# Attention contexts of a two-layer Flamingo block computed turned, four heads on column blocks of 32

## The reference

```python
x = x + tanh(g_xattn[0]) * L0_xattn(ctx, ctx, mask, layernorm(x), qc_score, ...)   # attention probabilities, 256 wide
x = x + tanh(g_ffn[0])   * L0_ffn(layernorm(x))      # shared expert + 8 experts, each run for all tokens, top 2 kept
x = x + tanh(g_xattn[1]) * L1_xattn(layernorm(x), ctx)
x = x + tanh(g_ffn[1])   * L1_ffn(layernorm(x))      # 8 experts, top 2 of 8
```

```python
scores  = einsum('bshr,bhlr->bhsl', q_r, k_r)          # queries and keys from folded weights
attn    = softmax(scores)                              # over the 256 latent rows l
ctx_c   = einsum('bhsl,bld->bhsd', attn, kv_rope)      # 64 values a head
ctx_lat = einsum('bhsd,hkd->bshk', ctx_c, w_kc_kv)
out     = ctx_lat.reshape(b, s, 16*128) @ Wo.T
```

## Time and profile before

| | |
|---|---|
| time, median of 3 runs | 470.16 us (469.36 to 470.41) |
| the profiled execution | 468.57 us, of which the span of the trace is 466.7 us |
| PE busy | 395.1 us, 85% of the span |
| PE's weight loads busy | 328.2 us, 70% |
| DVE busy | 261.4 us, 56% |
| ACT busy | 248.2 us, 53% |
| POOL busy | 135.8 us, 29% |
| mean granted TensorE clock | 0.955 of full speed |

### The profile page before, as it was taken

How to read it: one execution, slowest core, us unless ns; L and a number is a source line. 1 busy time by engine, 2 the same in 40 slices (tenths; PEclk the granted TensorE clock), 3 DMA queues, 4 the chain that set the end, 5 groups by cost and what they waited for, 6 DMA issues and landing times. The chain is left out here.

```text
span 466.7 us, 7900 instructions
## 1 busy us (share of the span) xinstructions
PE 395.1 (85%) x2691; PEld 328.2 (70%) x2691; DVE 261.4 (56%) x732; ACT 248.2 (53%) x507; POOL 135.8 (29%) x140
## 2 busy tenths in 40 slices
PE   1669994867988998898988898778998799999996
PEld 0335682456688777897778887678997677778885
DVE  0889434437623549624649433759762456555885
ACT  1013786437289466598484897543464354444331
POOL 4815100017001047011254011335178900001630
PEclk9999996958599999999999999999999899999999
DMA  5995700381001001020010100031264422211320
GB/s 156 303 328 186 103 2 0 117 266 44 2 23 25 2 22 25 2 47 1 1 46 3 24 23 2 1 97 47 63 204 145 146 89 73 90 46 58 103 91 23
DMA packets 30744, 35.37 MB, mean 76 GB/s; under 512 B 5713, under 2 KB 25793, under 8 KB 30449
## 3 DMA queue, kind: packets, MB, share of 16 engines
q1 hardware_dynamic: 26304, 28.11, 20.0%
q0 software_dynamic: 4400, 6.75, 6.4%
HBM read 25.61 MB, written 7.60 MB: 71 GB/s over the span
## 5 line engine op out<-in xcount | busy, mean ns | idle before, releaser
L1412 PE MATMUL bank<-kv,probs 128*128 128x128 f32 x512 | 67.6, 275 | 5.3 <-ACT negmT L1005 4.9
L1412 PEld LDWEIGHTS bank<-kv,probs 128*128 128x128 f32 x512 | 62.5, 192 | 6.2 <-issue 6.2
L1032 ACT ACTIVATE probs<-bank 128x512 f32<-128x512 f32 x64 | 37.5, 592 | 17.2 <-PE bank L1392 17.2
L1864 DVE TENSOR_REDUCE negm<-bank 128x2 f32<-128x512 f32 x64 | 41.4, 688 | 5.1 <-PE bank L1371 4.8
L1391 PE MATMUL bank<-Qs,Kh 128*128 128x256 f32 x128 | 39.0, 326 | 0.0
L1371 PE MATMUL bank<-Kh,Qs 128*128 128x256 f32 x128 | 32.3, 347 | 7.6 <-ACT fold_d L1015 3.0
L1574 PEld LDWEIGHTS bank<-W,hTs 128*128 128x128 f32 x210 | 28.1, 189 | 13.4 <-DVE hTs L2018 7.8
L936 ACT ACTIVATE gu_all<-bank 128x512 bf16<-128x512 f32 x44 | 25.9, 594 | 19.6 <-PE bank L1195 19.5
L1574 PE MATMUL bank<-W,hTs 128*128 128x256 f32 (+1 forms) x210 | 32.9, 293 | 3.8 <-DVE hTs L2018 2.6
L747 POOL TENSOR_TENSOR W<-w_in,W 128x512 fp32r<-128x512 f32 x24 | 30.0, 1279 | 21.2 <-issue 21.2
L736 POOL TENSOR_SCALAR veps<-mv 128x2 f32<-128x2 f32 x12 | 2.7, 225 | 111.2 <-DVE mv L1608 111.2
(11 more groups left out here) (209 smaller groups left out, 896.4 us busy)
## 6 DMA issues: line engine op xcount, KB each, us to landing
Qm<-Qs SPq DMA_DIRECT2D x32, 128.0 KB
xs<-f3A SPq DMA_DIRECT2D x1, 2432.0 KB, 10.2
Qm<-xs SPq DMA_DIRECT2D x19, 128.0 KB, 2.0
ys<-y SPq DMA_DIRECT2D x19, 128.0 KB, 2.0
w_q<-in_wq SPq DMA_DIRECT2D x2, 1024.0 KB, 17.8
w_o<-in_woT SPq DMA_DIRECT2D x1, 2048.0 KB, 11.2
w_in<-in_L_ffn_Wg SPq DMA_DIRECT2D x8, 256.0 KB, 4.6
w_in<-in_L_ffn_Wu SPq DMA_DIRECT2D x8, 256.0 KB, 3.1
```

The costliest lines, as they stand in the source:

```text
L1032: done(act.activation(flat(pT[:, n % 3]), bank1(b, FILL_ST + h)[:], ACT.Exp), "p_ready")
L1412: ins = pe.matmul(bank_v(b, h // 2)[:, at:at + P], pT[:, n % 3, lt, t * P:(t + 1) * P], kv_all[:, frm:frm + P], start=(lt == 0), stop=(lt ...
L1864: done(dve.tensor_reduce(negm[:, :, max_at(h)], rows(bank1(b, FILL_S + h)), AX.X, ALU.max, negate=True), "m_ready")
```

## The change

Contexts are computed turned. Exponentials now move, and the latent is stationary: for a quad of four heads, matmuls with 32 stationary columns go to output partitions 32k to 32k+31, one head k to each block. One round of them with a 128x32 block of ones gives each head's denominator, repeated on 32 partitions (`denominators(q)`); two rounds with the two halves of 32 of the latent's columns give the values (`values(q)`). A quad is 24 matmuls with 256 moving columns each. No transposes follow: DVE takes the reciprocal of 128x256 denominators into `rec`, multiplies 128x512 values with it and writes `full` in SBUF; ACT copies that once, into the high part. The second copy on ACT is gone; POOL (batch 3: DVE) makes the low part from `full`.

The quads stand at h5, h9, h13 and h17 on PE behind `scores_T` (the last denominators at h18 for batches 0 to 2), the reciprocal and the multiply at h6, h10, h14 and h18 on DVE, the high copy still at h7, h11, h15 and h19 on ACT. There are 6 buffers of exponentials in place of 3. Go, the folded output weights, is laid out by the same blocks: L1320 becomes 8 matmuls on blocks of 32 columns. In L1264 and L1265 the two heads of a pair now follow each other by operand (both first parts, then both second parts).

```diff
@@ PE: the fold
-                    for h in range(4 * q, 4 * q + 4):
-                        o = bank[4][half(h), h // 2 % 4 * KD:(h // 2 % 4 + 1) * KD]
-                        pe.matmul(o, w_qra[:, h], w_kqa[:, h], start=True, stop=False)
-                        ins = pe.matmul(o, w_qrb[half(h), h // 2], w_kqb[half(h), h // 2], start=False, stop=True)
+                    def o(h):
+                        return bank[4][half(h), h // 2 % 4 * KD:(h // 2 % 4 + 1) * KD]
+
+                    for pr in range(2 * q, 2 * q + 2):
+                        for h in (2 * pr, 2 * pr + 1):
+                            pe.matmul(o(h), w_qra[:, h], w_kqa[:, h], start=True, stop=False)
+                        for h in (2 * pr, 2 * pr + 1):
+                            ins = pe.matmul(o(h), w_qrb[half(h), pr], w_kqb[half(h), pr], start=False, stop=True)
...
-                    for j in range(2):
-                        for par in range(2):
-                            h = 2 * (2 * n + j) + par
-                            ins = pe.matmul(bank_go(n)[par * DC:(par + 1) * DC, j * H:(j + 1) * H], w_kv[:, h], w_o[:, h],
-                                            start=True, stop=True)
+                    for part in range(2):
+                        for k in range(4):
+                            ins = pe.matmul(bank_go(n)[QD * k:QD * k + QD, part * H:(part + 1) * H],
+                                            w_kv[:, 4 * n + k, part * QD:(part + 1) * QD], w_o[:, 4 * n + k], start=True, stop=True)
@@ PE: attn1
+                def in_quad(q, o, weights, sig):
+
+                    for lt in range(T):
+                        for k in range(4):
+                            ins = pe.matmul(o[QD * k:QD * k + QD], weights(lt), pT[(NH * b + 4 * q + k) % 6][:, lt],
                                             start=(lt == 0), stop=(lt == 1))
...
+                def denominators(q):
+
+                    pe.wait_ge(S_["p_ready"], NH * b + 4 * q + 4)
+                    if q:
+                        pe.wait_ge(S_["rec_ready"], NQ * b + q)
...
+                    in_quad(q, bank_den(b)[:, 0:S], lambda lt: ones[:], "den_ready")
+
+                def values(q):
+
+                    pe.wait_ge(S_["p_ready"], NH * b + 4 * q + 4)
...
+                    for part in range(2):
+                        in_quad(q, bank_v(b, q)[:, part * S:(part + 1) * S],
+                                lambda lt: kv[:, b * T + lt, part * QD:(part + 1) * QD], "pv_ready" if part else None)
...
-                    if 2 <= h <= NH + 1:
-                        values(h - 2)
-                    if h >= 7 and (h - 7) % 4 == 0:
-                        turn_ctx((h - 7) // 4)
+                    if h >= 5 and (h - 5) % 4 == 0:
+                        q = (h - 5) // 4
+                        if q < NQ - 1 or b == B - 1:
+                            denominators(q)
+                        values(q)
+                    if h == NH + 2 and b < B - 1:
+                        denominators(NQ - 1)
@@ ACT: attn1
-                        if n >= 3:
-                            act.wait_ge(S_["pv_ready"], n - 2)
+                        if n >= 6:
+                            act.wait_ge(S_["den_ready"], (n - 6) // 4 + 1)
+                            act.wait_ge(S_["pv_ready"], (n - 6) // 4 + 1)
...
-                        done(act.activation(flat(pT[:, n % 3]), bank1(b, FILL_ST + h)[:], ACT.Exp), "p_ready")
+                        done(act.activation(flat(pT[n % 6]), bank1(b, FILL_ST + h)[:], ACT.Exp), "p_ready")
...
-                        done(act.activation(flat(ctxs[:, 0, 2 * k:2 * k + 2]), bank_c(b)[:], ACT.Copy), "cT_hi")
-                        if b < B - 1:
-                            done(act.activation(wait_full(act, b, 4 + k), bank_c(b)[:], ACT.Copy), "cT_full")
+                        done(act.activation(flat(ctxs[:, 0, 2 * k:2 * k + 2]), full[k % 2], ACT.Copy), "cT_hi")
@@ DVE: attn1
-                    if h >= 3 and h % 2 and h <= NH + 1:
-                        pr = (h - 3) // 2
...
-                        done(dve.reciprocal(rden[:, m % 2], o[:, :, :, DC]), "pv_step")
-                        own(dve, "pv_step")
-                        done(dve.tensor_tensor(ctxn[:, :, 2 * pr:2 * pr + 2].rearrange("p t a d -> p a t d"), o[:, :, :, 0:DC],
-                                               rden[:, m % 2, :, :, None].to_broadcast([P, 2, T, DC]), ALU.mult), "ctx_ready")
+                    if h >= 6 and (h - 6) % 4 == 0:
+                        q = (h - 6) // 4
+                        m = NQ * b + q
+                        dve.wait_ge(S_["den_ready"], m + 1)
...
+                        done(dve.reciprocal(rec[:, m % 2], bank_den(b)[:, 0:S]), "rec_ready")
+                        dve.wait_ge(S_["pv_ready"], m + 1)
+                        own(dve, "rec_ready")
+                        done(dve.tensor_tensor(wait_full(dve, b, 4 + q).rearrange("p (a s) -> p a s", a=2),
+                                               bank_v(b, q)[:].rearrange("p (a s) -> p a s", a=2),
+                                               rec[:, m % 2, None, :].to_broadcast([P, 2, S]), ALU.mult), "ctx_ready")
```

More of the change, by code:

```diff
@@ L29 @@
 NP = NH // 2
+NQ = NH // 4
+QD = 32
 KD, CQ, R = 128, 192, 64
@@ L301, in passing @@
             return layer1.enter_context(nc.sbuf_tensor(name, shape, dt))
-        ctxn = passing("ctxn", [P, T, NH, DC])
+        probs_b = passing("probs_b", [P, 3 * T * S])
+        rec = passing("rec", [P, 2, S])
+        pT = [w[:, n * T * S:(n + 1) * T * S].rearrange("p (t s) -> p t s", t=T) for w in (probs, probs_b) for n in range(3)]
         ctxs = passing("ctxs", [P, 2, NP, S], F32R)
@@ L482, in wait_full, with bank_v, bank_den @@
                 pb, k = divmod(n, SPLITS)
-                if k < 4:
+                if k < 4 and pb < B - 1:
                     eng.wait_ge(S_["q_split"], 8 * pb + 2 * (k + 1))
+                elif k < 4:
+                    eng.wait_ge(S_["cT_lo"], NQ * pb)
                 else:
-                    eng.wait_ge(S_["cT_lo"], 4 * pb + k - 3)
+                    eng.wait_ge(S_["cT_lo"], NQ * pb + k - 3)
             return full[(SPLITS * b + i) % 2]
[L489 to L495, removed]
+        def bank_v(b, q):
+            return bank[(7, 4 if b < B - 1 else 3)[q % 2]]
+        def bank_den(b):
+            return bank[0 if b < B - 1 else 4]
         def qm_at(h):
@@ L789, in rotate @@
                 cv, rv, kvv = (w.rearrange("p (b t) c -> p b t c", b=B) for w in (cx, rot, kv))
-                done(pool.memset(kv[:, :, DC:DC + 1], 1.0), "rope_step")
-                done(pool.memset(kv_all[:, B * T * (DC + 1):], 0.0), "rope_step")
+                done(pool.memset(ones[:], 1.0), "rope_step")
                 done(pool.tensor_tensor(rv[:, :, :, 0:h2], cv[:, :, :, h2:DC], tab(sin, 0, h2), ALU.mult), "rope_step")
@@ L1393, in scores_T @@
                     done(ins, "sT_ready")
[L1395 to L1408, removed]
-                        for lt in range(T):
-                            at, frm = (h % 2 * T + t) * P, (b * T + lt) * (DC + 1)
-                            ins = pe.matmul(bank_v(b, h // 2)[:, at:at + P], pT[:, n % 3, lt, t * P:(t + 1) * P], kv_all[:, frm:frm + P],
-                                            start=(lt == 0), stop=(lt == 1))
-                    done(ins, "pv_ready")
-                def turn_ctx(k):
-                    pe.wait_ge(S_["ctx_ready"], NP * b + 2 * k + 2)
-                    if k:
-                        ctx_left(pe, 4 * b + k)
-                        if k == 3 and b < B - 2:
+                def in_quad(q, o, weights, sig):
+                    for lt in range(T):
+                        for k in range(4):
+                            ins = pe.matmul(o[QD * k:QD * k + QD], weights(lt), pT[(NH * b + 4 * q + k) % 6][:, lt],
+                                            start=(lt == 0), stop=(lt == 1))
+                    if sig:
+                        done(ins, sig)
+                def denominators(q):
+                    pe.wait_ge(S_["p_ready"], NH * b + 4 * q + 4)
+                    if q:
+                        pe.wait_ge(S_["rec_ready"], NQ * b + q)
+                        if q == NQ - 1 and b < B - 2:
                             pe.wait_ge(S_["fT0_sb"], b + 3)
@@ L1426, in turn_ctx @@
                         pe.wait_ge(S_["hsT_sb"], 2 * (b + 2))
-                    for j in range(2):
-                        for t in range(T):
-                            pr = 2 * k + j
-                            ins = pe.transpose(bank_c(b)[:, j * S + t * P:j * S + (t + 1) * P],
-                                               flat(ctxn[:, t, 2 * pr:2 * pr + 2]), ident[:])
-                    done(ins, "cT_ready")
+                    in_quad(q, bank_den(b)[:, 0:S], lambda lt: ones[:], "den_ready")
+                def values(q):
+                    pe.wait_ge(S_["p_ready"], NH * b + 4 * q + 4)
+                    if q == 0:
```

(11 more changed lines are left out.)

45 lines of the change are left out of this document (19 added, 26 removed).

## The result

The changed kernel takes 513.95 us (median of 4 runs, 512.5 to 514.76), the kernel before 469.76 us beside it: a ratio of 1.0963, 95% interval 1.0881 to 1.1044. The forecast was 489 us, with 507 as the upper end. The sign was right; the loss is 44 us in place of 19.

What follows compares the result with a forecast made beforehand. It took PE feeding ACT just in time to bound the loop, PE the down stage, a DVE chain the boundary. Terms of 15.85 us, 19.1 with the clock, took the profiled 468.57 to 487.7, median 489 us; range 463 to 507.

Steps and rivals of the forecast that it cites:

- Clock: PE's idle time before the down stage and fT0 widens; two half-speed stretches in all, 3.3 us (0 to 10).
- loop: Head loop, batches 0 to 2: ACT starves behind the quads at h5 and h9, +1.4 us a batch (-1.5 to +2.5).
- down stage and `y_sum`: Quad 2 falls in the PE-bound down stage, +1.05 us; its reciprocal and multiply on DVE delay `y_sum`, +2.2 us.
- boundary: Between batches: PE's values of quad 3 stand between fT0 and fT2 in place of later transposes, +0.1 us.
- high copy, queries, rows: Boundary: the last reciprocal and multiply follow `f2_lo` on DVE; ACT's high copy and query copies wait, +1.5 us.
- PE, a quad: PE's matmuls for one quad, four blocks abreast: 2.85 us, 1.1 us less than before.
- DVE, a quad: DVE's reciprocal of 128x256 for one quad: 2.0 us (0.42 to 1.95 from the rows), plus a 0.69 us multiply.
- Batch 3: +0.4: Last batch: PE's saving is hidden ahead of the scatter's landing; larger DVE pairs push the scatter 0.4 us (0 to 1.5).
- The fold: -1.7: Query fold L1264/L1265: paired halves save PE some 6 us, of which 1.7 us shows (0 to -2.3).
- PE sets the pace: Rival, 0.16: ACT stays fed through the quads and the reciprocal is near 0.42 us, so PE's saving counts: 455 us.
- blocks ran four abreast: Rival, 0.07, claimed they don't: a quad takes 5.4 us, 31 us more in 12 quads, some 520 us.
- reciprocal was not cheap: Rival, 0.20, claimed a cheap one: `y_sum` loses only 0.65 us, the queries nothing; 478 us, up to 480.

Runs made afterwards that it cites:

- a_filled: Changed kernel plus spare matmuls in PE's waits ahead of h3, h4, h5, h8, the down stage, fT0 and three row scores: 499.87 us.
- a_filled_b3: Changed kernel with spare matmuls in PE's waits, also in the last batch (ahead of its queries, h2 to h5 and the output): 494.42 us.
- a_oldfold: Changed kernel with the query fold L1264/L1265 back in its former head-by-head order: 514.84 us.
- a_spread_cheap: Changed kernel with each quad's rounds on three heads (last quad of a batch whole) and a copy for the reciprocal: 481.95 us.
- b_filled2: Kernel before plus spare matmuls in PE's waits of the fold, batch 0, batch 2's last transposes and the tile stage: 460.74 us.
- a_spread: Changed kernel with each quad's rounds on three heads (last quad whole), 7 exponential buffers, multiply and high copy two steps later: 491.24 us.
- a_spread_filled: Changed kernel with each quad's rounds on three heads (last quad whole) plus spare matmuls in PE's waits: 497.7 us.
- a_spread_cheap_filled: Changed kernel with quad rounds on three heads (last quad whole), a copy for the reciprocal and spare matmuls in PE's waits: 488.23 us.

## Why the prediction was wrong

The step that failed is the one it called *Clock*: "I take two such stretches in all, 3.3 us (0 to 6 of them, 10 us)". There were 24 more than before. Holding the clock with spare work brings 513.95 down to 494.42 us, so this term is at least 19.5 us, since the spare work costs something too and 55 us at half clock are still left, where the kernel before has 44. It named two idle places a batch; it missed the third and fourth (PE waiting for exponentials at h3 to h5, which it no longer fills with values of its own, and the row scores behind the late high copy). Above all it did not follow a fall into the work behind it: the quad stands behind the first of these waits, takes some 5.1 us in place of 2.6 at half clock (its first and last fours start at 138.47 and 143.16 us in batch 0, 0.43 apart), and in batch 1 ACT waits 4.25 us behind it.

With the clock held, the other steps of batch 1 came out near their sizes:

| step | forecast | change | a_filled |
|---|---|---|---|
| loop | +1.4 | +3.4 | +1.2 |
| down stage and `y_sum` | +1.05 + 2.2 | +4.5 | +2.9 |
| boundary | +0.1 | +1.9 | 0.0 |
| high copy, queries, rows | +1.5 | +3.8 | +3.1 |
| sum | 6.25 | 13.6 | 7.2 |

*PE, a quad*: 2.6 us for the forecast 2.85; right. *DVE, a quad*: 1.75 us for 2.0, near enough; its price against a copy, 2.6 us a batch where no half speed stands on either side, is 2.8 by the forecast's steps (1.3 us ahead of `y_sum`, 1.5 behind `f2_lo`). The last row of the table is larger than forecast; three pairs of spare matmuls stand in that stage. With the copy and no spare work it takes 22.7 us, as before; with the copy and the spare work 23.8. So some 1.1 of the 3.1 us are the spare work's and 2.0 the reciprocal's, for the forecast 1.5.

Over the whole run the pieces of a_filled_b3, cut at each `y_sum`, are -0.5, +4.5, +7.1, +7.7 and +5.2 us against before, where the forecast without its clock has -1.7, 4.65, 6.25, 6.25 and 0.4: 24 us for 15.85. Most of the difference is the last piece.

*Batch 3: +0.4* failed as a term: it is 7.1 us, 4.7 with most of the half speed there gone. The step said that PE's saving "is hidden" behind the scatter and looked only at what the routing waits for; it did not ask what the contexts' own chain does where no feed-forward block stands beside it. With two arms of about equal end, only one was followed. From the last `y_sum` to h0 of batch 3 another 1.9 us were lost (33.1 us before, 35.0 after). The sum gives this boundary nothing; what the 1.9 us are was not separated from the clock, which ran 14 us at half speed there, 3.4 before. *The fold: -1.7* came to nothing. PE's saved time became idle time there, and half speed followed; that the clock took the gain back is not shown, since a_oldfold, at full clock in that place, is neither faster nor slower.

The rivals: "PE sets the pace" did not come about, though a quad takes PE less time; ACT's waits inside the loop, the point from which it decides, grew from 1.0 to 4.5 us in batch 1. The blocks ran four abreast, and the reciprocal was not cheap.

What stays open: in the best form with the changed passes (a_spread_cheap, without a division) 12.8 us against before remain, 4.6 of them in the last batch. Its half-speed stretches still come to 79 us; how much of the rest is theirs was not settled. Nor is the split of the 44 us into clock and waits closed: with spare work on both sides (494.42 us against b_filled2's 460.74) the change still costs 34 us, but 55 us at half speed are left on one side and 3 on the other.

## What to carry to other kernels

Saving time on PE was worth nothing by itself here, where PE waits for ACT and DVE: the saved time turned into idle time, and idle time can be paid for twice, once as a wait and once as the lower clock of what runs behind it. So read the granted clock beside each wait that a change widens, and look at what stands right behind that wait. In a tuned kernel the waits that already run into half clock are worth a few spare matmuls, sized to the wait and put in free banks: that alone gave 1.7% here. Spare matmuls sized for the changed kernel's waits cost 6 us once its quads were spread.

## What the runs showed of the hardware

Four fp32 matmuls on column blocks of 32 with different moving operands run fully side by side: 0.22 us from one four to the next with 256 columns, as for a single one before (0.216), with a change of layout that costs about 0.1 us (0.33 us from the last four of the quad above to the next gu step).

A subtraction on DVE with both operands in SBUF can wait for POOL. In a_spread the low part of the last batch took 3.35 us where its neighbour took 0.63; POOL's three products W ran beside it (timeline of DVE, then of POOL, same kernel):

```profile
366.46 0.63 DVE L1882 TENSOR_TENSOR ctxs<-fT,ctxs 128x512 fp32r<-128x512 f32 x1
...
372.69 3.35 DVE L1882 TENSOR_TENSOR ctxs<-fold_d,ctxs 128x512 fp32r<-128x512 f32 x1
```

```profile
371.73 3.74 POOL L746 TENSOR_TENSOR W<-w_in,W 128x512 fp32r<-128x512 f32 x3
```

In two other kernels it took 4.43 us (a_spread_filled) and 4.35 us (a_spread_cheap_filled) beside these products, and in the changed kernel 1.00 us beside the end of one such product. Before, the same subtraction read one operand from a bank and took 0.69 us throughout, also beside a product (353.38 to 354.65 us); the change moved that operand to SBUF. The Trainium skill, page "SBUF — State Buffer", section "Terms", says that DVE and GpSimd hold a shared pair of ports for a whole instruction and the loser blocks; the two rows agree: the subtraction ends at 376.04 us, its own 0.6 us after POOL's third product.
